# A linear-attention and Hadamard-FFN block: seven block products for the down projection of the third and fourth pair of chunks

## The reference

```python
xn = layernorm(x)
q, k, v = (xn @ W.T + b for W, b in ((Wq, bq), (Wk, bk), (Wv, bv)))
phi_q, phi_k = elu(q) + 1, elu(k) + 1
kv_sum = cumsum(phi_k * v, axis=1)                  # over the tokens of a chunk
s = (phi_q * kv_sum * SCALE) @ Wo.T + bo

y = fwht(xn * SU_ug) / 64                           # Walsh-Hadamard over 512
h = silu(y @ W_gate.T * scale) * (y @ W_up.T * scale)   # 2048 hidden features
g = silu(fwht(h * SU_dp) / 64 @ W_down.T * scale)
out = x + s * g
```

## Time and profile before

| | |
|---|---|
| median of 3 runs | 1308.63 us (1308.14 to 1309.26) |
| span of the profiled execution, its time | 1308.6 us |
| TensorE busy | 1276.1 us (98%), 5968 matmuls |
| VectorE busy | 886.8 us (68%) |
| ScalarE busy | 589.3 us (45%) |
| GpSimd busy | 59.1 us (5%) |
| granted TensorE clock, mean | 0.998 of full |
| DMA | 212.03 MB, mean 162 GB/s |

### The profile page before, as it was taken

How to read it: one execution, slowest core, us unless ns; L and a number is a source line. 1 busy time by engine, 2 the same in 40 slices (tenths; PEclk the granted TensorE clock), 3 DMA queues, 4 the chain that set the end, 5 groups by cost and what they waited for, 6 DMA issues and landing times.

```text
span 1308.6 us, 16031 instructions
## 1 busy us (share of the span) xinstructions
PE 1276.1 (98%) x5968; PEld 578.5 (44%) x5968; DVE 886.8 (68%) x1367; ACT 589.3 (45%) x880; POOL 59.1 (5%) x101
## 2 busy tenths in 40 slices
PE   5999999999999999999999999999999999999998
PEld 3544444444444444444444444444444444444443
DVE  6989999977756777777664755566762774555721
ACT  5875566631235655552324554442333654443220
POOL 1000101212000000110000000010000000000000
PEclk9999999999999999999999999999999999999999
DMA  9512552668764456653554323334453323323340
GB/s 374 212 65 89 174 188 113 216 243 286 207 251 149 145 207 239 206 185 129 193 193 161 129 97 129 112 147 161 161 195 129 126 99 127 119 107 112 114 156 37
DMA packets 56957, 212.03 MB, mean 162 GB/s; under 512 B 12208, under 2 KB 14512, under 8 KB 40368
## 3 DMA queue, kind: packets, MB, share of 16 engines
q1 hardware_dynamic: 45872, 179.55, 38.2%
q0 software_dynamic: 7536, 25.70, 5.8%
q10 hardware_dynamic: 3472, 5.77, 1.3%
HBM read 164.83 MB, written 46.16 MB: 161 GB/s over the span
## 4 chain that ended last, share of the span: by engine, by line
PE 58%; DVE 2%; issue 2%; ACT 2%; DMA 1%; DVEq 0%; ACTq 0%
PE bank L1875 39%; PE bank L1998 19%; DMA h_all<-scr_f 1%; DVE work L1261 1%; ACT work L922 1%; DVE work L1277 1%; ACT work L925 1%; DVE work L1267 0%; DVE h_all L1311 0%; DVE work L1302 0%; ACT work L905 0%; ACT L922 0%; DVE h_all L1424 0%; DVE h_all L1425 0%; DVE h_all L1601 0%
## 5 line engine op out<-in xcount | busy, mean ns | idle before, releaser
L1875 PE MATMUL bank<-xops,ring 128*128 128x512 f16 x2772 | 602.6, 379 | 8.6 <-DVE work L1261 3.3
L1875 PEld LDWEIGHTS bank<-xops,ring 128*128 128x128 f16 x2772 | 269.5, 98 | 340.6 <-issue 10.2
L1998 PE MATMUL bank<-h_all,ring 128*128 128x512 f16 x1536 | 333.8, 379 | 1.8 <-DMA ring<-scr_d 1.4
L1261 DVE TENSOR_TENSOR work<-bank,work 128x512 f32<-128x512 f32 x198 | 133.5, 686 | 163.2 <-PE bank L1875 150.5
L1998 PEld LDWEIGHTS bank<-h_all,ring 128*128 128x128 f16 x1536 | 149.9, 98 | 184.1 <-DVE work L1261 1.9
L1763 PE MATMUL bank<-xops,ring 128*128 128x512 f16 x1008 | 226.2, 381 | 2.5 <-DVE ring L1405 2.5
L905 ACT ACTIVATE work<-bank 128x512 f32<-128x512 f32 x198 | 117.8, 595 | 231.0 <-PE bank L1875 231.0
L1763 PEld LDWEIGHTS bank<-xops,ring 128*128 128x128 f16 x1008 | 98.4, 98 | 126.6 <-issue 10.5
L947 ACT ACTIVATE h_all<-work 128x512 f16<-128x512 f32 x128 | 78.1, 624 | 72.0 <-DVE work L1302 69.3
L1311 DVE TENSOR_TENSOR h_all<-work,h_all 128x512 f16<-128x512 f32 x128 | 87.4, 685 | 8.6 <-ACT h_all L947 7.5
L1267 DVE SCALAR_TENSOR_TENSOR work<-work 128x512 f32<-128x512 f32 x64 | 44.1, 689 | 49.7 <-ACT work L925 49.4
(11 more groups left out here) (210 smaller groups left out, 1023.0 us busy)
## 6 DMA issues: line engine op xcount, KB each, us to landing
ring<-scr_g SPq DMA_DIRECT2D x72, 1024.0 KB, 4.9
ring<-scr_d SPq DMA_DIRECT2D x32, 1024.0 KB, 5.4
scr_g<-ring SPq DMA_DIRECT2D x22, 512.0 KB, 3.3
h_all<-in_ug_t SPq DMA_DIRECT2D x8, 1024.0 KB, 12.3
x_res<-in_x_t SPq DMA_DIRECT2D x32, 256.0 KB, 4.3
out<-x_res SPq DMA_DIRECT2D x32, 256.0 KB, 4.4
scr_g<-ring POOLq DMA_DIRECT2D x12, 512.0 KB, 4.0
work<-in_x_t SPq DMA_DIRECT2D x6, 1024.0 KB, 7.3
```

The source lines that it names most:

```text
L1261: dve.tensor_tensor(tile(g, j), at[:, :], tile(g, j), ALU.add).then_inc(summed, 1)
L1875: mm = pe.matmul(to[:, :], weight_of(slot, s, b, kk), at, start=(a == 0 and m in (P1, P2, P5)), stop=(a == 5), skip_group_check=True)
L1998: mm = pe.matmul(d_bank(c, t)[:, :], w[:, t, ws, :], at[:, s, :], start=(a == 0 and b == 0 and n == 0), stop=(a == KB - 1 and b == KB - 1 ...
```

## The change

In pairs 3 and 4 the down projection too is computed with seven block products, for hidden pieces 0 to 5 of 8 (`SEVEN` = 6); pieces 6 and 7 are plain products (`rest`), added into the same banks. Both chunks are done at once, and the two Wo groups come last.

- Weights: `down_high` also stores the unsplit down weights (`scr_df`). Six units (`UNITS`) of sums S1 to S4 are made at the turn from pair 2 to pair 3: `load_unit` and `store_unit` (GpSimd's DMAs), `unit_add` and `unit_low` (VectorE), `unit_high` (ScalarE), into `scr_s`. All of down now has one scale, so the norms of all four quarters are taken first (`load_probe`, `square_down` at tiles 15, 16, 19, 20), and quarters 0 and 1 are loaded after that.
- Hidden sums: for pieces 0 to 5, `hidden_sums` (VectorE, four subtractions), `hidden_sums_high` (ScalarE) and `hidden_sums_low` (VectorE) make T1 to T4.
- Ring: four slots in pairs 3 and 4. Slot 0 and parts of `work`, `x_res` and `gates` hold hidden sums.
- Outputs: VectorE multiplies by the attention output (`gated`), GpSimd adds the tokens (`add_tokens`), 8 tiles in a pair. Four of them stand in `seven_and_o`, the other four in groups 0 and 1 of the next pair, or at the end.
- The statistics of the fourth pair's tokens are taken in groups 8 and 10 instead of 16 and 18.

```diff
-RING = (1, 2, 3, 4, 0)
+RING, LATER_RING = (1, 2, 3, 4, 0), (1, 2, 3, 4)
+SEVEN_FROM, SEVEN = 2, 6
+DOWN_SLOTS = (P1, P2, P6, P7, P5, R11, P4, P3)
+DOWN_ORDER = [(d, m) for ms in ((P1, P2), (P6,), (P7,), (P5,), (R11,), (R21,), (R22,), (R12,), (P4,), (P3,))
+              for d in range(2) for m in ms]
+PROBE, SQUARE_DOWN_AT = (2, 3, 0, 1), (15, 16, 19, 20)
-FLY_DOWN_AT, SCALE_DOWN_AT = (0, 1, 2, 3), 4
+FLY_DOWN_AT, SCALE_DOWN_AT = (1, 2, 3, 4), 4
...
 gpsimd, pair p:
+                if p >= SEVEN_FROM:
+                    for n in range(8):
+                        add_tokens(p, n)
+                if p == SEVEN_FROM - 1:
+                    load_unit(0)
+                    load_unit(1)
+                    for u in range(UNITS):
+                        store_unit(u)
+                        if u + 2 < UNITS:
+                            load_unit(u + 2)
...
 scalar, group():
                 copy_sum(p, g, 1)
+                if g >= 2 and in_seven(p, g - 2):
+                    hidden_sums_high(p, (g - 2 - QKV_GROUPS) // 2)
...
                 take(p, g, C11)
+                if p == SEVEN_FROM and g < UNITS - 4:
+                    unit_high(4 + g)
...
 scalar, second pair, second chunk:
-                if p < PAIRS - 1:
-                    x_high(p + 1, 0)
-                    t_high(p + 1, 0)
-                    x_high(p + 1, 1)
-                    t_high(p + 1, 1)
+                x_high(p + 1, 0)
+                t_high(p + 1, 0)
+                unit_high(0)
+                x_high(p + 1, 1)
+                unit_high(1)
+                t_high(p + 1, 1)
+                unit_high(2)
+                unit_high(3)
                 silu_outs(2 * p + 1)
...
 vector:
+            def hidden_sums(p, i, part):
+                ...
+                if part == 0:
+                    dve.wait_ge(h_made, 32 * p + 4 * i + 4)
+                    prep.after(dve.tensor_tensor(b12, b12, b11, ALU.subtract))
+                    prep.after(dve.tensor_tensor(b22, b22, b12, ALU.subtract))
+                else:
+                    dve.tensor_tensor(b11, b22, b11, ALU.subtract)
+                    dve.tensor_tensor(b21, b21, b22, ALU.subtract).then_inc(hidden_summed, 1)
...
 vector, group():
+                if p > SEVEN_FROM and g < 2:
+                    pair_outputs(p - 1, (4 + 2 * g, 5 + 2 * g))
+                if p == SEVEN_FROM and g < UNITS - 4:
+                    unit_add(4 + g)
+                    unit_low(3 + g)
+                    if g == UNITS - 5:
+                        unit_low(4 + g)
...
 tensor:
+            def seven(p, d, m):
+                ...
+                for i in range(SEVEN):
+                    for n, (s, xs) in enumerate(((HI, HI), (HI, LO), (LO, HI))):
+                        ...
+                        mm = pe.matmul(to[:, :], down_weight(slot, d, i, s), at,
+                                       start=(i == 0 and n == 0 and m in (P1, P2, P5)),
+                                       stop=(i == SEVEN - 1 and n == 2), skip_group_check=True)
```

More of the change, by code:

```diff
@@ L79 @@
 C11, C22, C21, C12 = range(4)
+GATE_ORDER = [(d, j) for j in (C11, C22, C21, C12) for d in range(2)]
+OUT_ORDER = [(d, j) for d in range(2) for j in (C11, C22, C21, C12)]
 PLAIN_BANKS = (0, 1, 2, 3)
@@ L255, in gate_of, with ct_sum @@
                 return gates[:, t, :]
-            return h[:, t, c % 2, :, :].rearrange("p s n -> p (s n)").bitcast(F32)
+            if c >= 2 * SEVEN_FROM:
+                d, r = t % 2, t // 2
+                return down_tile(d, ((C11, C12), (C21, C22))[r][c % 2])
+            return h_tile(t, c % 2)
+        def ct_sum(p, n):
+            return h_tile(n, 2) if p >= SEVEN_FROM else gates[:, n, :]
         def stage(q):
@@ L1900, in group @@
                     product(p, g, P3)
+                elif g + 1 == GROUPS and p >= SEVEN_FROM:
+                    seven(p, 0, P1)
+                    product(p, g, P4)
+                    product(p, g, P3)
+                    for d, m in DOWN_ORDER[1:]:
+                        if m < R11:
+                            seven(p, d, m)
+                        else:
+                            rest(p, d, m)
                 elif g + 1 == GROUPS:
@@ new lines, in rest @@
+            def rest(p, d, m):
+                n = GROUPS + DOWN_SLOTS.index(R11)
+                slot = slot_of(p, n)
+                r, c = {R11: (0, 0), R21: (1, 0), R22: (1, 1), R12: (0, 1)}[m]
+                if m == R11:
+                    pe.wait_ge(slot_loaded[slot], 16 * loads_into(p, n))
+                    pe.wait_ge(h_ready, 32 * p + 4 * FP)
+                elif m == R21:
+                    pe.wait_ge(seven_copied, down_copied_to(p, d, P7))
+                elif m == R12:
+                    pe.wait_ge(seven_summed, down_summed_to(p, d, "22a"))
+                elif p == SEVEN_FROM:
+                    pe.wait_ge(gate_ready, 8 * p)
+                else:
+                    pe.wait_ge(seven_summed, down_summed_to(p - 1, d, "22"))
+                to = {R11: right_bank(d), R21: chain_bank(d), R22: bank[REST_BANKS[d]], R12: left_bank(d)}[m]
+                terms = [(i, half, s, xs) for i in range(SEVEN, FP) for half in range(2)
+                         for s, xs in ((HI, HI), (HI, LO), (LO, HI))]
+                for n, (i, half, s, xs) in enumerate(terms):
+                    mm = pe.matmul(to[:, :], rest_weight(slot, half, d + 2 * r, i, s), h[:, i, 2 * half + c, xs, :],
+                                   start=(m == R22 and n == 0), stop=(n == len(terms) - 1), skip_group_check=True)
+                mm.then_inc(seven_done, 1)
```

542 lines of the change are left out of this document (444 added, 98 removed).

## The result

| | before | changed |
|---|---|---|
| median of 4 runs each | 1308.95 us (1308.14 to 1309.70) | 1324.15 us (1322.90 to 1325.00) |
| span of the profiled execution | 1308.6 us | 1322.4 us |
| matmuls | 5968 | 5896 |

The changed kernel is slower: ratio 1.0117, 95% interval 1.0102 to 1.0131. I had predicted 1314 (1301 to 1322): the sign was right, the size was not. The medians differ by 15.2 us.

The account below looks back on a forecast made before the run. TensorE's number of matmuls was taken to bound the kernel. The terms -15.5 + 0 + 0 + 2.0 + 3.0 + 3.7 + 4.2 + 1.5 + 1.5 + 4.9 = +5.3 gave 1314 us, range 1301 to 1322.

Parts of the forecast that it names:

- the -15.5: Down projections of pairs 3 and 4: 72 fewer matmuls at 0.2158 us each save 15.5 us.
- Rival D: Gate/up groups of pairs 3 and 4: VectorE binds them, 6 us on top, 1320 us; chance 0.12.
- The turn: Pair 2 to 3 and groups 0, 1: unit work delays TensorE by 3.0, 3.7 and 4.2 us, 10.9 in all.
- Rival A: Whole kernel: the matmuls win; turn costs 3 us, tail 4, rest 1, giving 1301 us; chance 0.18.
- B: Whole kernel: rival of near a draw, half of the turn's 10.9 us paid, 1308.5 us; chance 0.18.
- The first weights for down: Before the first down matmul: the new 1 MB store of unsplit weights delays the last down store, +2.0 us (0 to 2.8).
- Start-up: Early norms of the down weights: 0 us, between -4 (2.5 us stall gone) and +4 (ScalarE later).
- P5's load: Third pair's down: P5's weights load behind the mean store and spread, so its product waits +1.5 us (0 to 3).
- the tail: After the last matmul: one sum, four gatings, four GpSimd additions and a store take 9.7 us, +4.9.
- The start of pair 4: Groups 0 and 1: four gatings and a held load against silus and outputs gone, +1.5 us (-0.5 to +5).
- rival C: Start of pair 4 and tail: GpSimd and VectorE block each other, 2 x 1.3 plus 2 us, 1318.5 us; chance 0.12.
- The clock: Behind three or four stalls of 3 to 4 us TensorE may run slow, +1.7 each, up to +6, outside the sum.

Follow-up runs that it names:

- all_moved: Changed kernel with units_mid, all_on_vector and outs_late edits, P5's load ahead of the tokens, and fourth-pair outputs made as each tile is there: 1296.70 us, ratio 0.9906 to before.
- Units_late: Changed kernel with sums of units 3, 4 and 5 moved to the ends of third-pair groups 2, 5 and 6, copy and split one group later: 1313.46 us.
- units_mid: units_late_slots with sums and splits of units 3, 4, 5 in mid-group, fourth pair's statistics in groups 10 and 12: 1310.29 us, ratio 1.0007 to the kernel before.
- The two one-tile kernels: Kernel before with GpSimd adding the tokens to one tile: the very last (1314.85 us), or one of the seventh chunk some 45 us ahead of the end (1309.28 us).
- outs_late: all_on_vector with the third pair's last four gatings and additions one each in groups 1, 3, 4 and 6 of the fourth pair, their stores later: 1312.36 us.
- tail_on_vector: Changed kernel with the fourth pair's eight token additions on VectorE, not GpSimd: 1316.79 us, ratio 1.0051 to the kernel before.
- all_on_vector: Changed kernel with all sixteen token additions of both pairs on VectorE, none on GpSimd: 1316.40 us, ratio 1.0048 to the kernel before.
- the three units kernels: Changed kernel with units 3, 4 and 5 later: units_late (1313.46 us), units_late_slots (1311.79 us) and units_mid (1310.29 us).
- all_moved_gpsimd3: all_moved with the third pair's eight token additions on GpSimd again: 1296.34 us, ratio 0.9904 to the kernel before.
- units_late_slots: units_late with the four ring slots of pairs 3 and 4 used in the order 3, 4, 1, 2 instead of 1, 2, 3, 4: 1311.79 us.
- before_gpsimd_last: Kernel before with GpSimd instead of VectorE adding the tokens to the very last tile: 1314.85 us, ratio 1.0041.

## Why the prediction failed

**What held.** The bound (TensorE by its number of matmuls) and the -15.5: pair 4's down gave 8.1, and all_moved keeps 12.4 of it. VectorE's room in the gate/up groups: 13.4 to 14.2 us busy in three windows of 18.1 or 18.2 us from 817.2 on, against the 13.8 of 18.1 worked out, the wide copy of 128x1536 at 1.75 against 1.7, and no cost. Rival D is out. The turn: unit 3 was summed at 698.8, as walked through, and the silus ended at 702.2 (702.5). 3.67 us for unit 4's copy on ScalarE (I had 3.7); the late silus cost 2.3 (3.0). At the V tiles ScalarE was part of it again: 2.01 us of TensorE's wait are for a copy behind that of unit 5, then 0.99 for VectorE. In sum the waits were 9.0 us, 8.5 more than before, where I had 10.9, and the slow clock added 2.8: that the turn came out near my 10.9 is partly luck. Rival A, with 3 us for all of it, is out, and so is B, with half. Units_late and units_mid show the mechanism as I had it, edit by edit.

**The first weights for down: +2.0 predicted, nothing came.** TensorE's wait there is 1.4 us as before; the store of the unsplit weights delayed nothing. Start-up itself lost 1.4 us (four short waits and one stretch of slow clock for one long one), which I had at 0, and in these two profiles pair 2 gave it back, as its waits there are for weight sums that a transfer sets. That was luck of the profile of before. The two one-tile kernels have its code up to pair 3, and there that pair starts at 694.99 and 696.05, not at 697.67; in the nine kernels with the new start-up it starts at 696.5 to 698.0. By these the start costs about 1 us, which the table doesn't show and the medians do. So my equality of the span of 1308.6 with the median was wrong by some 1.5 us too.

**P5's load: +1.5 predicted, 1.58 measured, but not always.** The wait on `ring<-scr_s` is 0.48 in outs_late and absent in tail_on_vector, all_on_vector and the three units kernels, all with the same order of loads. So the hit is partly luck. The time of this transfer varies; I can't say by what, and no run moves this load alone.

**The step that failed most is the tail.** I wrote: "four times 1.27 + 0.1 gives 7.15, store 2.55: 9.7". Two things were wrong. The additions took 1.26 only where VectorE was idle; beside gatings 1.5 to 1.8, and the first waited for that of the tile before, so the last ended 9.3 us behind the last matmul. That is 2.1 us over the 7.15. And I let the store end the program, where GpSimd's DRAIN did: from the last addition to the end 5.6 us instead of 2.55. The second is the graver: the row of 6952 ns was in the trace of before, on GpSimd's queue, and I did not ask what an engine does after its last instruction when I made it the last to work. The pair of one-tile experiments shows it by itself.

**The start of pair 4: "2 x 0.69 in the gapless V stretch", +1.5, measured +6.4.** The gatings were priced, GpSimd's hold on VectorE (4.1 us) was left to rival C, and the clock to a sentence outside the sum. Rival C had the mechanism: the Trainium skill, SBUF — State Buffer ("Who interferes with whom"), says that a VectorE instruction with two inputs in SBUF and a GpSimd instruction that reads SBUF exclude each other. The trace agrees, with 3.44 us for 1.28; and an instruction of VectorE that takes a bank of PSUM and one tile of SBUF (with a factor per partition) is not held, as the same section would have it for a single SBUF input: in the tail, 0.75 us at 1304.92 in the middle of an addition.

```profile
1304.28 1.27 POOL L939 TENSOR_TENSOR h_all<-h_all,x_res 128x512 f32<-128x512 f32 x1 [0.17 <-POOL h_all L939]
...
1304.92 0.75 DVE L1581 SCALAR_TENSOR_TENSOR h_all<-bank,o_out,h_all 128x512 f32<-128x512 f32 x1 [1.27 <-PE bank L2320]
```

C's 2 us for the tail was right (the 2.1 us above). Its 2 x 1.3 for the start was too low against 4.1 us, since both engines lose; but all_on_vector shows that this hold was not what decided, and outs_late and all_moved_gpsimd3 that the place was: eight instructions, four of them GpSimd's, ahead of the V tiles, where VectorE has no slack.

**The clock.** "Up to +6, not in it": it was 2.6 us at the start of pair 4 and 2.8 at the turn (66 matmuls at 16.24 for 14.40, six at 2.44 for 1.47). A term that I expected "three or four" times at +1.7 belonged in the sum; in this profile it makes up 5.4 of the 8.5 us that the sum was short by, and lies within the lines of the turn and of the start of pair 4. But it is no fixed price. The start of pair 4 has the same code and the same wait of 3.65 us in five kernels, and the 66 matmuls behind it took 17.02 us in the changed kernel, 15.98 in tail_on_vector, 16.09 in units_late_slots and units_mid, and 14.40, so no loss at all, in units_late.

## What to carry to other kernels

An instruction costs by where it stands, not by how long it takes: units 3, 4 and 5 cost 11.9 us at the turn and in groups 0 and 1 (the slow clock behind their waits included), and about nothing in the middle of groups where VectorE waits for ScalarE. When work is given to an engine that had none at the end, look at what closes the program on that engine and count it behind its last instruction. When a stall is taken away, look for the transfer that was late behind it.

## What the runs showed of the hardware

- GpSimd's closing DRAIN ended 5.4 to 6.5 us behind its last tensor addition (6.7 us long in the changed kernel, 7.9 in the two one-tile kernels, begun as the addition begins), and where GpSimd worked last the program waited for it; VectorE's took 0.7 us in before_gpsimd_last and ended with its last gating.
- A GpSimd addition of 128x512 float32 takes 1.26 us alone, 1.83 times VectorE's 0.69, and 1.5 to 1.8 beside VectorE instructions with two SBUF inputs. Two of these took 3.44 us together in place of 1.28, and one in the tail 1.75 in place of 0.69.
- The slow clock does not follow from the length of the last wait. In the changed kernel the 42 matmuls behind the wait of 3.67 us took 9.35 us, as at full clock, and those behind the next two waits, 2.01 and 0.99 us, ran slow; in tail_on_vector, with the same code there and a wait of 3.63 us, the 42 took 10.67. Behind 3.65 us at the start of pair 4 the loss was 0 to 2.6 us; behind 2.35 us in units_late matmuls ran slow, behind 1.8 us in pair 2 they did not. The 42 in tail_on_vector, and the window behind the 2.01 in the changed kernel:

```profile
717.37 10.67 PE L2329 MATMUL bank<-xops,ring 128*128 128x512 f16 x42 [3.63 <-ACT work L1168]
```

```profile
730.00:732.00 2.00, 1.01 (x3) 0.13 (x2) 1.97 (x3) 0.60 (x1) 2.00 (x4) 0.50 0.87 295
```
